# Two heads interleaved in a scan's K, Q, turned and score blocks: 128-byte pieces in the spreads, an 8-byte step in the stationary operands

## The reference

```python
def step(carry, inp):                      # one chunk; W1c (16x16) and b1c (16) are the state of an image and head
    W1c, b1c = carry
    xq, xk, xv, et = inp                   # 16 tokens x 16 dims; xq, xk rotated (RoPE)
    Z1 = xk @ W1c + b1c
    grad = _ln_l2_bwd(Z1, xv - xk, g, bb)
    Attn1 = jnp.tril(xq @ xk.swapaxes(-1, -2))
    b1_bar = b1c - jnp.tril(et) @ grad
    Z1_bar = xq @ W1c - et * Attn1 @ grad + b1_bar
    last_eta = et[..., -1, :, None]
    W1n = W1c - (last_eta * xk).swapaxes(-1, -2) @ grad
    b1n = b1c - (last_eta * grad).sum(-2, keepdims=True)
    return ((W1n, b1n), xq + _ln(Z1_bar, g, bb, EPS_IN))
```

## Time and profile before

| | |
|---|---|
| median of 3 runs | 1993.09 us (1989.3 to 1993.84) |
| profiled execution | 1991.81 us, its span 1989.7 us |
| granted TensorE clock, mean | 0.643 of full speed |
| PE busy | 1620.6 us (81%), 33520 matmuls |
| PE weight loads busy | 1206.9 us (61%) |
| DVE busy | 1579.8 us (79%) |
| ACT busy | 991.3 us (50%) |
| POOL busy | 1315.9 us (66%) |
| DMA packets | 1650518, of them under 512 bytes 1630176 |

### The profile page before, as it was taken

How to read it: one execution, slowest core, us unless ns; L and a number is a source line. 1 busy time by engine, 2 the same in 40 slices (tenths; PEclk the granted TensorE clock), 3 DMA queues, 4 the chain that set the end, 5 groups by cost and what they waited for, 6 DMA issues and landing times.

```text
span 1989.7 us, 82066 instructions
## 1 busy us (share of the span) xinstructions
PE 1620.6 (81%) x33520; PEld 1206.9 (61%) x33520; DVE 1579.8 (79%) x3721; ACT 991.3 (50%) x2358; POOL 1315.9 (66%) x1479
## 2 busy tenths in 40 slices
PE   1886978922798889888888888888888898888886
PEld 1443544511676667767667667667676676676674
DVE  6999997704788788888888887887888887888864
ACT  2223545443455555555555555555555555555553
POOL 1244535365687787777777777777777777777763
PEclk9997999965555655555555556655566555655555
DMA  6058696963465665675665665665656656666554
GB/s 238 1 30 45 97 97 68 81 148 69 52 76 68 71 80 69 74 78 67 73 79 68 73 73 70 76 72 68 80 65 73 79 68 72 73 70 76 67 61 49
DMA packets 1650518, 148.80 MB, mean 75 GB/s; under 512 B 1630176, under 2 KB 1643744, under 8 KB 1650144
## 3 DMA queue, kind: packets, MB, share of 16 engines
q1 hardware_dynamic: 1390640, 117.87, 51.0%
q10 hardware_dynamic: 259504, 25.70, 10.7%
HBM read 40.71 MB, written 38.54 MB: 40 GB/s over the span
## 4 chain that ended last, share of the span: by engine, by line
SPq 24%; PE 16%; DVE 15%; DMA 10%; issue 7%; ACT 3%; DVEq 0%; POOL 0%; ACTq 0%; POOLq 0%
SPq L477 16%; DMA kqk<-work 8%; SPq L493 7%; PE p_kt L1624 6%; PE p_x L1668 4%; DVE work L1303 2%; DMA late<-work 2%; DVE work L1270 2%; DVE work L1294 2%; PE p_m L1653 2%; DVE work L1363 1%; PE p_x L1659 1%; DVE work L1385 1%; DVE zs L1350 1%; DVE m L1357 1%
## 5 line engine op out<-in xcount | busy, mean ns | idle before, releaser
L795 ACT ACTIVATE work<-p_kt 128x512 f16<-128x512 f32 x196 | 149.1, 761 | 213.7 <-PE p_kt L1624 212.9
L1624 PEld LDWEIGHTS p_kt<-fold,kqk 128*128 128x128 f16 x6272 | 185.0, 104 | 97.2 <-ACT work L795 46.1
L1624 PE MATMUL p_kt<-fold,kqk 128*128 128x16 f16 x6272 | 200.6, 175 | 52.8 <-DMA kqk<-work 45.0
L1597 PE MATMUL p_j<-wa,work 128*128 128x512 f16 x196 | 119.5, 610 | 146.9 <-DVE work L1270 102.2
L621 POOL TENSOR_TENSOR work<-work,rope_s 128x256 f32<-128x256 f32 x196 | 161.5, 844 | 83.8 <-DVE work L1270 83.8
L592 POOL TENSOR_TENSOR work<-work,g 128x256 f32<-128x256 f32 x98 | 71.8, 732 | 201.7 <-DVE work L1341 198.8
L1303 DVE TENSOR_TENSOR work<-work 128x256 f16<-128x256 f32 x196 | 164.3, 893 | 15.8 <-ACT work L782 15.8
L1532 PE MATMUL p_j<-work 128*128 128x392 f16 x864 | 157.7, 344 | 23.3 <-DVE work L1117 20.7
L1668 PEld LDWEIGHTS p_y<-w,late 128*128 128x128 f16 x4704 | 145.7, 103 | 17.9 <-issue 8.5
L1668 PEld LDWEIGHTS p_x<-w,late 128*128 128x128 f16 x4704 | 149.0, 105 | 12.3
L1597 PEld LDWEIGHTS p_j<-wa,work 128*128 128x128 f16 x196 | 24.9, 127 | 207.4 <-issue 176.6
(11 more groups left out here) (173 smaller groups left out, 4397.4 us busy)
## 6 DMA issues: line engine op xcount, KB each, us to landing
kqk<-work SPq DMA_DIRECT2D x392, 64.0 KB, 4.7
late<-work SPq DMA_DIRECT2D x392, 64.0 KB, 3.8
late<-work SPq DMA_DIRECT2D x392, 32.0 KB, 2.6
out_y<-work ACTq DMA_DIRECT2D x49, 256.0 KB, 6.8
x_scratch<-late SPq DMA_DIRECT2D x24, 392.0 KB, 11.8
xs_scratch<-work SPq DMA_DIRECT2D x24, 392.0 KB, 6.5
work<-x_scratch ACTq DMA_DIRECT2D x49, 192.0 KB, 3.6
work<-xs_scratch SPq DMA_DIRECT2D x48, 192.0 KB, 2.8
```

What stands on the lines that cost most here:

```text
L795: return act.activation(kqt16[:, o, g:g + GP, :, :, :].rearrange("p g h t a -> p g a (h t)"), p_kt[:, :].rearrange("p (g a n) -> p g a n", ...
L1597: pe.matmul(p_j[k][:, 0:4 * C], tokens(s, k, 0), wa16[:, :], start=True, stop=False, skip_group_check=True)
L1624: mm = pe.matmul(p_kt[:, at:at + CS], part_of(g + k, h, a), fold16[:, :], start=True, stop=True)
```

## The change

Two heads that stand next to each other (2s and 2s+1) are interleaved. The innermost axes of all four tiles and their block-diagonal destinations were (dim or token, half); now they are (dim or token, half, head of the pair). A piece of a spread, 16 dims or tokens with all that belongs to them, is then 16 x 2 x 2 x 2 bytes = 128 bytes instead of 64, and there are half as many: 512 in a transfer of 64 KB, 256 in one of 32 KB. Transfers, bytes, waits and the orders of all engines stay as they are. A stationary operand (one half of one head) steps 4 elements, 8 bytes, instead of 2, 4 bytes, over all its 128 columns; so do the 16 moving columns of k_dot_q. ACT and DVE write the tiles with a step of 8 bytes in runs of 16, and the fold puts its results into `p_kt` in the new order (head pair, half, head), so that ACT still reads the bank in order.

```diff
+HP = NH // 2
...
-        mbd = second.cut([NG, NH, GB, CS, 2], F16)
-        ktqt1 = second.cut([2, NG, NH, GB, CS, 2], F16)
+        mbd = second.cut([NG * HP, GB, CS, 2, 2], F16)
+        ktqt1 = second.cut([2, NG * HP, GB, CS, 2, 2], F16)
...
-        kq_sets = [kqk[:, 0:2 * third].rearrange("p (s b e) -> p s b e", b=GB, e=2 * HD),
+        kq_sets = [kqk[:, 0:2 * third].rearrange("p (s b e) -> p s b e", b=GB, e=4 * HD),
...
-        hl16 = scan.cut([2, 2, NG, C, 2], F16)
+        hl16 = scan.cut([2, 2, NG * HP, HD, 2, 2], F16)
...
-        kqt16 = scan.cut([2, NG, NH, CS, 2], F16)
-        mc16 = scan.cut([NG * C, 2], F16)
+        kqt16 = scan.cut([2, NG * HP, CS, 2, 2], F16)
+        mc16 = scan.cut([NG * HP, CS, 2, 2], F16)
...
+        def split(ap):
+            return ap.rearrange("p (s j d) -> p s j d", j=2, d=HD)
+
+        def half_of(c, at, g, a):
+            return hl16[:, c % 2, at, g * HP:(g + GP) * HP, :, a, :].rearrange("p s d j -> p s j d")
...
-                part = hl16[:, c % 2, :, :, :, :].rearrange("p o g (h d) a -> p (o g h) (d a)", d=HD)
+                part = hl16[:, c % 2, :, :, :, :, :].rearrange("p o s d a j -> p (o s) (d a j)")
...
-                part = kqt16[:, :, :, :, :, :].rearrange("p o g h t a -> p (o g h) (t a)")
-                whole = ktqt[c % 2][:, :, :, :, :, :, :].rearrange("p o g h b t a -> p (o g h) b (t a)")
+                part = kqt16[:, :, :, :, :, :].rearrange("p o s t a j -> p (o s) (t a j)")
+                whole = ktqt[c % 2][:, :, :, :, :, :, :].rearrange("p o s b t a j -> p (o s) b (t a j)")
...
-                part = mc16.rearrange("p (s t) a -> p s (t a)", t=CS)
-                whole = mbd.rearrange("p g h b t a -> p (g h) b (t a)")
+                part = mc16.rearrange("p s t a j -> p s (t a j)")
+                whole = mbd.rearrange("p s b t a j -> p s b (t a j)")
...
-                    last = act.activation(hl16[:, c % 2, at, g:g + GP, :, 0], pair(qk[:, o, :]), ACT.Copy)
+                    last = act.activation(half_of(c, at, g, 0), split(qk[:, o, :]), ACT.Copy)
...
-                return act.activation(kqt16[:, o, g:g + GP, :, :, :].rearrange("p g h t a -> p g a (h t)"),
-                                      p_kt[:, :].rearrange("p (g a n) -> p g a n", g=GP, a=2), ACT.Copy)
+                return act.activation(kqt16[:, o, g * HP:(g + GP) * HP, :, :, :].rearrange("p s t a j -> p s (a j) t"),
+                                      p_kt[:, :].rearrange("p (s x t) -> p s x t", x=4, t=CS), ACT.Copy)
...
-                act.activation(mc16[:, :, 0], p_m[:, :], ACT.Copy).then_inc(m_high_done.sem, 1)
+                act.activation(mc16[:, :, :, 0, :].rearrange("p s t j -> p s j t"),
+                               p_m[:, :].rearrange("p (s j t) -> p s j t", j=2, t=CS), ACT.Copy).then_inc(m_high_done.sem, 1)
...
-                    last = dve.tensor_tensor(hl16[:, c % 2, at, g:g + GP, :, 1], pair(qk[:, o, :]),
-                                             hl16[:, c % 2, at, g:g + GP, :, 0], ALU.subtract)
+                    last = dve.tensor_tensor(half_of(c, at, g, 1), split(qk[:, o, :]), half_of(c, at, g, 0), ALU.subtract)
...
-                dve.tensor_tensor(mc16[:, :, 1], p_m[:, :], mc16[:, :, 0],
-                                  ALU.subtract).then_inc(m_low_done.sem, 1)
+                dve.tensor_tensor(mc16[:, :, :, 1, :].rearrange("p s t j -> p s j t"),
+                                  p_m[:, :].rearrange("p (s j t) -> p s j t", j=2, t=CS),
+                                  mc16[:, :, :, 0, :].rearrange("p s t j -> p s j t"), ALU.subtract).then_inc(m_low_done.sem, 1)
...
-                return blocks[:, k_of[c % 2], g, h, :, :, a].rearrange("p b d -> p (b d)")
+                return blocks[:, k_of[c % 2], g * HP + h // 2, :, :, a, h % 2].rearrange("p b d -> p (b d)")
...
-                return ktqt[c % 2][:, o, g, h, :, :, a].rearrange("p b t -> p (b t)")
+                return ktqt[c % 2][:, o, g * HP + h // 2, :, :, a, h % 2].rearrange("p b t -> p (b t)")
...
-                            at = ((k * 2 + a) * NH + h) * CS
+                            at = ((k * HP + h // 2) * 4 + 2 * a + h % 2) * CS
...
-                            mm = pe.matmul(p_m[:, at:at + CS], kq_turned(c, 1, g, h, a), kqt16[:, 0, g, h, :, w],
+                            mm = pe.matmul(p_m[:, at:at + CS], kq_turned(c, 1, g, h, a), kqt16[:, 0, g * HP + h // 2, :, w, h % 2],
...
-                            mm = pe.matmul(p_y[:, at], mbd[:, g, h, :, :, a].rearrange("p b t -> p (b t)"), g16[:, p, w, at],
+                            mm = pe.matmul(p_y[:, at], mbd[:, g * HP + h // 2, :, :, a, h % 2].rearrange("p b t -> p (b t)"), g16[:, p, w, at],
```

More of the change, by code:

```diff
@@ L163, in program @@
         second = Carver(late)
-        mbd = second.cut([NG, NH, GB, CS, 2], F16)
-        ktqt1 = second.cut([2, NG, NH, GB, CS, 2], F16)
-        ktqt0 = second.cut([2, NG, NH, GB, CS, 2], F16)
+        mbd = second.cut([NG * HP, GB, CS, 2, 2], F16)
+        ktqt1 = second.cut([2, NG * HP, GB, CS, 2, 2], F16)
+        ktqt0 = second.cut([2, NG * HP, GB, CS, 2, 2], F16)
         ktqt = [ktqt0, ktqt1]
         third = 4 * NH * GB * 2 * HD
-        kq_sets = [kqk[:, 0:2 * third].rearrange("p (s b e) -> p s b e", b=GB, e=2 * HD),
-                   kqk[:, third:3 * third].rearrange("p (s b e) -> p s b e", b=GB, e=2 * HD)]
-        blocks = kqk[:, :].rearrange("p (o g h b d a) -> p o g h b d a", o=3, g=NG, h=NH, b=GB, a=2)
+        kq_sets = [kqk[:, 0:2 * third].rearrange("p (s b e) -> p s b e", b=GB, e=4 * HD),
+                   kqk[:, third:3 * third].rearrange("p (s b e) -> p s b e", b=GB, e=4 * HD)]
+        blocks = kqk[:, :].rearrange("p (o s b d a j) -> p o s b d a j", o=3, s=NG * HP, b=GB, a=2, j=2)
         k_of = [0, 2]
@@ L557, in _ @@
             pool.wait_ge(xs_a.sem, xs_a.count("whole", 3 * GB - 1))
-            pool.memset(ktqt0.rearrange("p o g h b t a -> p (o g h b t a)"), 0.0).then_inc(s_kt_zero[0], 1)
+            pool.memset(ktqt0.rearrange("p o s b t a j -> p (o s b t a j)"), 0.0).then_inc(s_kt_zero[0], 1)
             for b in range(B - GB, B):
@@ L1250, in zero_late @@
                 dve.wait_ge(s_x2[3], 16)
-                dve.memset(ktqt1.rearrange("p o g h b t a -> p (o g h b t a)"), 0.0).then_inc(s_kt_zero[1], 1)
-                dve.memset(mbd.rearrange("p g h b t a -> p (g h b t a)"), 0.0).then_inc(s_m_zero, 1)
+                dve.memset(ktqt1.rearrange("p o s b t a j -> p (o s b t a j)"), 0.0).then_inc(s_kt_zero[1], 1)
+                dve.memset(mbd.rearrange("p s b t a j -> p (s b t a j)"), 0.0).then_inc(s_m_zero, 1)
             @guard
@@ L1576, in k_block @@
             def k_block(c, g, h, a):
-                return blocks[:, k_of[c % 2], g, h, :, :, a].rearrange("p b d -> p (b d)")
+                return blocks[:, k_of[c % 2], g * HP + h // 2, :, :, a, h % 2].rearrange("p b d -> p (b d)")
             def q_block(g, h, a):
-                return blocks[:, 1, g, h, :, :, a].rearrange("p b d -> p (b d)")
+                return blocks[:, 1, g * HP + h // 2, :, :, a, h % 2].rearrange("p b d -> p (b d)")
             def kq_turned(c, o, g, h, a):
-                return ktqt[c % 2][:, o, g, h, :, :, a].rearrange("p b t -> p (b t)")
+                return ktqt[c % 2][:, o, g * HP + h // 2, :, :, a, h % 2].rearrange("p b t -> p (b t)")
             @guard
```

## The result

The changed kernel takes 2096.39 us (median of 3 runs, 2095.65 to 2096.60) where the one before takes 1993.09: ratio 1.0537, 95% interval [1.0508, 1.0566]. The forecast was 1940, range 1885 to 2040, with 0.24 for slower. The profiled execution took 2096.6 us, its span is 2094.8.

A forecast was written before the change was run, and what follows sets the result against it. It took several almost equally long chains to bound the kernel, the spreads last; 1.5 - 0.3 - 0.1 = 1.1 us a chunk, times 48 = 53 us, gave 1991.8 - 53 + 1 = 1940 us, range 1885 to 2040.

The forecast's parts named there:

- The spreads: K/Q and turned block transfers in half the pieces: 4.5 us less each, of which 1.5 us a chunk reaches the end.
- the score row: Profile row of score transfers, 512 pieces each: eight issued in 6.5 us, landing 2.6 us after issue; taken for the new spreads.
- rival 3: The spreads' whole chain share comes off: 4.5 us a chunk, 1776 us; 0.05 for more gain than the likeliest, toward this.
- Weight loads: 608 small matmuls a chunk on PE load at 8 bytes instead of 4; taken to cost nothing, upper bound 53 ns each.
- rival 1: Weight loads at 8 bytes are slower, 2590 us if twice as long; in full or nearly, half of the 0.24 for slower.
- mild case: 1997 to 2100 us, half of the 0.24: loads a few ns longer, or 128-byte pieces taking twice as long, with surcharges.
- The rule of the Trainium skill: SBUF access needs two hits per 16-byte line for full bandwidth; 8-byte fp16 steps give exactly two, so taken as safe.
- ACT's copies: Turned copy writing at 8 bytes: 0.15 us more each on 761 ns, at most 0.25; 0.3 us a chunk.
- Which copies count: Two of four turned copies a chunk: both K copies, queued on ACT ahead of the root that DVE's 12 us wait for.
- The 3.8 us to spare: Slack forecast for the turned spread once K/Q blocks come sooner; Q copies end ahead of it, so were not counted.
- DVE: Subtractions qk_low and m_low reading and writing fp16 at 8 bytes: 0.1 us a chunk, at most 0.4, counted whole.
- Sum: 1.5 gained less 0.3 for copies and 0.1 for DVE: 1.1 us a chunk, times 48 periods 53 us, giving 1940.

The follow-up runs named there:

- experiment 9: Two kernels, each the kernel before with some writes at 8 bytes: turned copy alone, 2067.33 us (1.0390); qk_high, qk_low, m_high, m_low alone, 2002.94 us (1.0056).
- experiments 5 and 6: The kernel before with the scan's stationary operands read at a step of 16 bytes, 2777.43 us (one execution), and contiguously at 2 bytes, 1994.22 us (0.9992).

## Why the prediction was wrong

- **The spreads**: right. Mechanism and size held: issues at 0.64 us, landing 3.4 where 2.6 was taken from the score row, waits gone, 60 us for a forecast 72, and rival 3, the whole share of the chain, did not come.
- **Weight loads**: "I take nothing" is the step that failed most. Measured: 33.3 ns for 26.7, 4.1 us a chunk of work, of which 2.3 reached the end, 5.5 points in the kernel with cheap spreads. The place was seen, and rival 1 gave the point from which it decides, 28.3 ns; but it got too small a chance, and half of that for a load twice as long. Its own rule with 6.7 ns a load, 1992 + 48 x (4.1 - 1.1), gives 2136. That the measured 2096 lies in its mild case (1997 to 2100) is in part luck: PE's idle time took up nearly half of the loads' cost, and the copies cost more than the rule had for them. The reason given for nothing was that the load at full clock took the same 96 ns at 4 bytes as contiguous, so that an 8-byte step at half clock would ask for no more bytes per ns. But a load's duration in a row is not the distance between loads. At 1.00 loads start 25.0 ns apart, not half of 26.7, so the 4-byte step had been shown only up to 512 bytes (128 columns x 4) in 25 ns. At 8 bytes and half clock 1024 bytes in 26.7 ns would be needed, nearly twice that; 1024 in 33.3 is what came. The same rows read by their distance would have left the question open.
- **The rule of the Trainium skill** ("SBUF — State Buffer", section "Specifications (TRN2)") on two hits in each line put the change on the safe side. The measurement decides: at two hits a line the loads took 33.3 ns for 25.0 or 26.7, not full rate.
- **ACT's copies**: this term was mis-sized. 0.15 us was taken, bounded above by 0.25; it was 0.58. The bound came from going from contiguous to 4 bytes once (0.24 ns an element) and allowing twice that; from 4 to 8 bytes it was 1.1 ns an element. A surcharge measured at one step does not bound the next.
- **Which copies count**: the number, two, came out right for the changed kernel, but by luck. The two are not both K copies ahead of DVE's root: the chain after has the second K copy and the first Q copy on it, between folds that share p_kt, and PE stands for each. With late spreads (experiment 9) it is three, both Q copies among them. The 3.8 us to spare were spare only for the spread, not for PE.
- **DVE**: 0.1 us a chunk was forecast, at most 0.4; m_low alone took 0.60 more, the four qk_low 0.14 each, 1.2 us together. DVE's busy time a chunk stayed at 24.9 us all the same, as forecast: three other lines (L1350, L1363 and L1369 of the kernel before) took 0.6 less, which is half of it, and why they did stays open. What these writes and ACT's qk_high and m_high cost together was 12 us (experiment 9), with the short pieces left in; in the changed kernel it was not measured apart.
- **Sum** with the measured terms: 1.5 a chunk gained, and 608 x 6.7 ns = 4.1 and two copies, 1.2, lost would give 30.2 + 3.8 = 34. The period is 32.2: PE is busy 3.8 us longer a chunk, and its idle time took up 1.8 of it, falling from 3.6 to 1.8. So adding costs to the period was itself a step too simple: a cost on an engine with idle time is paid only in part.

## What to carry to other kernels

A layout has three customers, the transfer, the writer and the reader, and each has its own price for a step: price all three by rows of the very step, or measure each alone, since these traces said nothing of a step that the kernel did not use. Read the rate of weight loads from the distance of their starts in a long run at both clock levels, not from their duration. Where a copy must scatter, let it walk the destination in the order of memory and the source with the step: here that took a PSUM copy from 1337 to 597 ns, with the cost of the stepped read, if any, in the 597.

## What the runs showed of the hardware

- fp16 stationary operands of 128 columns, loads and 16-column matmuls in a run: 2 and 4 bytes of step the same, 25.0 ns apart at a granted clock of 1.00 and 26.7 at 0.50 (experiments 5 and 6); 8 bytes 33.3 at both; 16 bytes about 60 at both, by the starts in the traces. What sets 33 and 60 ns stays open; it is not the array's clock.
- ACT, 512 fp32 columns of PSUM to fp16: 597 ns in the order of memory, 761 at a step of 4 bytes, 1337 at 8. DVE's subtraction of the same size: 654 in runs of two elements, 723 at 4 bytes, 1320 at 8.
- DMA within SBUF, 16 partitions to a transfer, K/Q: 64 KB in 1024 pieces of 64 bytes take 1034 ns to issue in the median and land 4.7 us later, in 512 pieces of 128 bytes 642 ns and 3.4. The score spread, 32 KB, goes from 632 ns and 2.6 us with 512 pieces to 609 and 2.2 with 256. So the issue hardly gains below 512 pieces, and at 512 twice the bytes land 0.8 us later.
